# A gated feed-forward layer's up products on one core: the sigmoid goes ahead of the next unit's gate levels, and ScalarE makes the sigmoid's whole levels in every second unit

## What is computed

```python
def _L0_ffn_ref(x, w_gate, w_up, w_down):
    def act_qdq(x):                         # 16 bits, one scale for the whole tensor
        scale = jnp.maximum(jnp.max(jnp.abs(x)) / 32767.0, 1e-12)
        return jnp.clip(jnp.round(x / scale), -32768.0, 32767.0) * scale
    def fixed_qdq_u16(x):
        scale = 1.0 / 65536.0
        return jnp.clip(jnp.round(x / scale), 0.0, 65535.0) * scale
    x = act_qdq(x)
    up = act_qdq(x @ lpbq_dequant(w_up).T)
    gate = act_qdq(x @ lpbq_dequant(w_gate).T)
    sig = fixed_qdq_u16(jax.nn.sigmoid(gate))
    gate = act_qdq(gate * sig)
    o = act_qdq(gate * up)
    return o @ lpbq_dequant(w_down).T
```

## Time and profile before

| | |
|---|---|
| median of three runs | 1704.43 us (1702.17 to 1707.84) |
| profiled execution, its own time | 1706.82 us |
| its span in the profile | 1705.0 us |
| stretch of the gate products | about 379 to 447 us |
| stretch of the up products (16 units) | about 449 to 569 us |
| block `go` | about 571 to 629 us |
| mean granted TensorE clock, whole span | 0.848 |

### The profile page before, as it was taken

How to read it: one execution, slowest core, us unless ns; L and a number is a source line. 1 busy time by engine, 2 the same in 40 slices (tenths; PEclk the granted TensorE clock), 3 DMA queues, 4 the chain that set the end, 5 groups by cost and what they waited for, 6 DMA issues and landing times. The chain is left out here.

```text
span 1705.0 us, 29650 instructions
## 1 busy us (share of the span) xinstructions
PE 1293.8 (76%) x8779; PEld 956.2 (56%) x8780; DVE 1082.7 (64%) x1994; ACT 782.0 (46%) x1138; POOL 527.4 (31%) x426
## 2 busy tenths in 40 slices
PE   5779999349865008679969999533249999999996
PEld 3337777234322007526527777432239999999895
DVE  6947777685587784335647778567635555555553
ACT  0545665055555677100447777343424343444441
POOL 1046777000000000100037777244522333333333
PEclk9979999669999558855779999755569999999998
DMA  5000000100122440140002222384622322222221
GB/s 189 1 4 1 0 0 0 56 1 0 55 111 111 170 144 1 29 111 0 0 28 87 86 86 77 102 280 148 209 95 45 49 39 46 44 48 46 46 44 12
DMA packets 64938, 110.87 MB, mean 65 GB/s; under 512 B 9904, under 2 KB 50960, under 8 KB 64240
## 3 DMA queue, kind: packets, MB, share of 16 engines
q1 hardware_dynamic: 50576, 93.27, 17.3%
q0 software_dynamic: 14304, 16.87, 5.7%
HBM read 74.10 MB, written 37.83 MB: 66 GB/s over the span
## 5 line engine op out<-in xcount | busy, mean ns | idle before, releaser
L1810 POOL DMA_INDIRECT out<-ex_yo,ex_mt x78 | 137.3, 1760 | 314.4 <-DVE ex_yo L1785 181.4
L1735 ACT ACTIVATE ex_hT<-ex_ps_h,e_b1T,e_unscale 128x256 f32<-128x256 f32 x312 | 150.5, 563 | 115.9 <-PE ex_ps_h L1693 115.9
L549 PE MATMUL at_ps_s<-c_M,at_xnT_hi 128*128 (+1 forms) x512 | 163.1, 402 | 20.6 <-issue 13.5
L571 PE MATMUL at_ps_y<-c_VW,at_pT_hi 128*128 (+1 forms) x1024 | 171.1, 273 | 1.3 <-DVE main_x_res L669 1.3
L1693 PE MATMUL ex_ps_h<-ex_xT_hi,e_w_hi 128*128 128x256 f16 x624 | 171.1, 274 | 0.0
L1693 PE MATMUL ex_ps_h<-ex_xT_lo,e_w_hi 128*128 128x256 f16 x624 | 171.0, 274 | 0.0
L1693 PE MATMUL ex_ps_h<-ex_xT_hi,e_w_lo 128*128 128x256 f16 x624 | 171.0, 274 | 0.0
L1706 PE MATMUL ex_ps_y<-e_w_hi,ex_hT_lo 128*128 x624 | 170.1, 273 | 0.0
L1706 PE MATMUL ex_ps_y<-e_w_lo,ex_hT_hi 128*128 x624 | 170.1, 273 | 0.0
L1706 PE MATMUL ex_ps_y<-e_w_hi,ex_hT_hi 128*128 x624 | 170.1, 273 | 0.0
L641 DVE TENSOR_REDUCE at_mx<-at_sc 128x16 f32<-128x960 f32 (+1 forms) x96 | 80.0, 861 | 116.3 <-ACT at_sc L602 116.3
(11 more groups left out here) (273 smaller groups left out, 2914.0 us busy)
## 6 DMA issues: line engine op xcount, KB each, us to landing
at_half<-in_L_ffn_W SPq DMA_DIRECT2D x32, 512.0 KB, 3.6
rt_stage<-in_L_ffn_W SPq DMA_DIRECT2D x32, 512.0 KB
up_scratch<-gm_stg SPq DMA_DIRECT2D x16, 768.0 KB, 3.2
gm_stg<-up_scratch SPq DMA_DIRECT2D x16, 768.0 KB, 4.3
ex_row<-xs SPq DMA_DIRECT2D x39, 258.0 KB, 2.7
main_x_res<-in_x SPq DMA_DIRECT2D x8, 512.0 KB, 12.2
out<-main_x_res SPq DMA_DIRECT2D x4, 1024.0 KB
xs<-rt_pad SPq DMA_DIRECT2D x18, 129.0 KB
```

The costliest lines, as they stand in the source:

```text
L549: last = nc.tensor.matmul(ps_s[j][:, c * CH:(c + 1) * CH], a[:, d, :], b[:, d, bass.ds(off + c * CH, CH)], start=(n == 0), stop=(n == 3 * ...
L571: last = nc.tensor.matmul(ps_y[:, 0:D], a[j][:, n, :], b[:, bass.ds(off + n * D, D)], start=(n == 0 and i == 0), stop=(n == NP - 1 and i = ...
L1735: last = nc.scalar.activation(hT[:, n, :], ps_h[:, n, :], ACT.Relu, bias=b1T[:, bass.ds(e * HT + n, 1)], scale=unscale[:, 0, bass.ds(e, 1)])
L1810: nc.gpsimd.indirect_dma_start(out=acc[:, :], out_offset=bass.IndirectOffsetOnAxis(ap=mt[j][:, q, 1:2].bitcast(U32), axis=0), in_=yo[j][:, ...
```

## The change

ScalarE's order in the up products becomes up_out(u), sigmoid(u), in odd units `sig_levels(u)`, levels(u+1). `sig_levels` exists twice now: on VectorE for even units, as before, and on ScalarE for odd units, as a Copy of `unit(u)` with a constant scale of 65536 to `sq[1]`, without the explicit minimum, reported by a semaphore of its own, `sqa_r`. The product waits for `sq_r` in even units and for `sqa_r` in odd ones, with counts that go up once in two units.

```diff
+            sqa_r = z.sem("sqa_r")
...
+                def sig_levels(u):
+                    act.wait_ge(sig_r, u + 1)
+                    nc.scalar.activation(sq[u % 2][:, :], unit(u), ACT.Copy, scale=65536.0).then_inc(sqa_r, 1)
+
...
                 for u in range(NU):
                     up_out(u)
+                    sigmoid(u)
+                    if u % 2:
+                        sig_levels(u)
                     if u + 1 < NU:
                         levels(u + 1)
-                    sigmoid(u)
...
                 def product(u):
-                    dve.wait_ge(sq_r, u + 1)
+                    dve.wait_ge((sq_r, sqa_r)[u % 2], u // 2 + 1)
...
                 for u in range(NU):
                     up_max(u)
-                    sig_levels(u)
+                    if u % 2 == 0:
+                        sig_levels(u)
                     if u:
                         prod_max(u - 1)
                     product(u)
```

## The result

The changed kernel took 1676.45 us as the median of three runs (1675.28 to 1678.9), against 1704.43 before: a ratio of 0.9836 with a 95% interval of 0.9805 to 0.9868. It is faster, by 28.0 us. The profiled execution took 1675.28 us, its span is 1673.4 us.

The account below looks back on a forecast made before the run. It took a 7.40 us per-unit loop of waits across engines in the up products as the bound; saving 2.8 + 25.1 + 0.9 = 28.8 us from the 1704.43 us median gave 1675.6 us, range 1671 to 1684.

Parts of the forecast that it names:

- The loop of one unit: Up products before the change: waits from gate levels through sigmoid, sigmoid levels, product maximum and product, 7.40 us a unit.
- VectorE is the limit at 10.86 us for two units: Up products after the change: six instructions at 1.665 us plus one sigmoid-level at 0.87, 5.43 us a unit.
- two-unit loops of 7.9 and 8.9 us: Longest waits across engines after the swap: 7.9 us for odd u+1, 8.9 for even, both below VectorE's two-unit work.
- ScalarE is 0.6 us short of it: Up products: ScalarE's gate levels, up_out and sigmoid twice plus one copy need 10.3 us for two units, against VectorE's 10.86.
- The copy takes 1.57 us: ScalarE's new sigmoid-level Copy: 1.57 us, low end 1.52, high end 2.85 with a 1.28 us table load.
- TensorE and the stores are hidden: Up products: matmul groups of 4.06 us and stores of 3.2 us, one every 5.4 us, cost nothing.
- The sum: 2.8 + 25.1 + 0.9 = 28.8 us: Along VectorE in the up products: savings of 2.8 us at the start, 25.1 in the middle, 0.9 at the end.
- All of it reaches the end: Later stages start behind a barrier, so the whole 28.8 us carries to the kernel's end, giving 1675.6 us.
- Rival 1: Up products: costlier copy or hand-offs make ScalarE the limit, 11.6 us for two units, some 1681 us; chance 0.06.
- Rival 2: Up products: TensorE at 1.2 GHz, 7.69 us a group, only 4 us saved, 1700.5 us; chance 0.04.
- Rival 3: Second attention stage: started earlier, it runs at half the clock; 40 us of such work gives 1716 us; chance 0.02.
- Rival 4: Up products: gate levels behind the copy hold up the bank hand-off, only 7 us won, 1697 us; chance 0.03.

Follow-up runs that it names:

- the order alone: Against the kernel before: sigmoid(u) placed ahead of levels(u+1) on ScalarE, VectorE keeping all 16 sigmoid levels; stage 96.78 us, median 1676.03 us, ratio 0.9846.
- the move alone: The changed kernel with ScalarE's old order, levels(u+1) ahead of sigmoid(u), odd units' sigmoid levels still on ScalarE; stage 111.58 us, median 1690.26 us, ratio 0.9932.
- every third unit on VectorE: The changed kernel with VectorE making sigmoid levels only in units 0, 3, ..., 15, ScalarE in the others; stage 90.98 us, ratio 0.9812.
- even units shared with GpSimd: The changed kernel with even units' sigmoid levels split, GpSimd making the first 768 columns, VectorE the last 768; stage 89.42 us, ratio 0.9809.

## Why the prediction was right

1. *The loop of one unit is the limit.* Right. With the order alone changed it is gone (96.78 us), with it kept it stands (111.58 us).
2. *Afterwards VectorE is the limit at 10.86 us for two units.* Right: 10.84 us without idle time, up maxima 5.86 and 4.98 us apart. The two-unit loops of 7.9 and 8.9 us weren't tested by themselves.
3. *ScalarE is 0.6 us short of it.* Right in the sum: 0.50 us of idle time in two units, and a second copy cost 0.87 us of its 1.5. But two terms were off and cancelled, which is luck. The prediction charged nothing for the copy's wait for the sigmoid just ahead of it, "the sigmoid waits that way for the gate levels today". It doesn't: `sigmoid(u)` waits for gate levels u, which ScalarE made a unit earlier, and not for the gate levels u+1 just ahead of it. In the rows above the copy starts 510.31 - 508.71 = 1.60 us after the sigmoid, where it was taken as 1.47, and gate levels start 511.70 - 510.31 = 1.39 us after the copy, where it was taken as 1.5. With only the first off, ScalarE would have had 0.1 us less of its 0.6 us.
4. *The copy takes 1.57 us.* Wrong by 0.09, without effect on the sum, since ScalarE isn't the limit: it took 1.48, below the low end of 1.52 that I gave. The table load of the high end didn't come: the stage has one, ahead of the first sigmoid. The Trainium skill (ScalarE: Activation LUTs, "What ACT_TABLE_LOAD costs") gives 186 ns + 0.833 ns a column for immediate scale and bias and some 93 ns more for each scale or bias read from memory; an estimate from it is 1.47 us for this copy, and the trace agrees (1.48, against 1.56 to 1.58 for gate levels with a scale from memory).
5. *TensorE and the stores are hidden.* Right. No up_out in the stage had idle time ahead of it, so none waited for a store or for matmuls. All 13 groups behind the first three took 4.06 us. One pair of rows from TensorE's timeline, to set beside the earlier trace rows:

```profile
508.86 4.06 PE L934 MATMUL gm_bank<-f_xq,f_WuT 128*128 x18 [0.83 <-ACT gm_stg L972]
514.82 4.06 PE L934 MATMUL gm_bank<-f_xq,f_WuT 128*128 x18 [1.90 <-ACT gm_stg L972]
```

   The Trainium skill's rule on the clock (TensorE: Matmul & The Clock Gate, "A second HAM failure mode: psum-queue depth-cycling") fits the kernel before, where 4 of 13 groups were slow, but isn't borne out after the change: with idle times of 0.22 to 1.90 us between groups that take turns at the banks, none of the 13 groups was slow.
6. *The sum: 2.8 + 25.1 + 0.9 = 28.8 us.* The stage is 28.82 shorter. By parts, counted from gate levels 0: the up maximum of unit 2 starts 2.76 us earlier (17.45 before, 14.69 now), the 13 units take 96.11 - 70.92 = 25.19, and the end 5.98 - 5.11 = 0.87.
7. *All of it reaches the end.* It did: 28.0 us between the first medians. That the median of 1676.45 lies only 0.9 us from the forecast is in part luck, since on the other chips the same kernel had medians of 1669.11 to 1675.05 and gains of 25.4 to 30.9 us; the stage is the sharper test. The 2.5 us more in the span of the trace arose in later stages (the down products took 1.0 us less, the stretch from them to the end of the second attention 1.3 less), where the change does nothing; the spread of the runs is as large.

Rival 1 (ScalarE becomes the limit) didn't occur; a second copy and a copy in every unit each brought it about. Rival 2's price of 1700.5 us was for a case that wasn't run: it counts 13 groups and leaves the first three at 2.4 GHz, as they ran before (54 matmuls in 11.82 us). With all 16 at 7.77 us the kernel is slower (1.0039), so a low clock from the first group on would have cost more than the rival charges. That this clock didn't come is shown by two windows, up to TensorE's last group and behind it (columns of the earlier trace rows): the clock was 1.00 as long as there were matmuls.

```profile
449.00:523.00 74.00, 57.82 (x260) 24.05 (x258) 70.25 (x46) 72.25 (x51) 0.00 (x0) 1.00 0.37 149
523.00:540.00 17.00, 0.77 (x4) 0.16 (x2) 16.97 (x11) 9.94 (x7) 0.00 (x0) 0.60 0.23 93
```

Rival 3 (a later stage at a lower clock) isn't seen in any of the four traces of the change: the second attention has a granted clock of 1.00 in every window of 20 us from 900 to 1040 us, and ends some 1052 us into the first of them. Rival 4 (the change doesn't do what it says) falls with the stage's 28.82 us.

## What to carry to other kernels

When no engine of a stage is saturated, look for the loop that closes across engines, and ask of each member whether the next one needs it or only stands behind it: here an instruction for the *next* unit stood ahead of one that this unit waited for, and swapping the two brought four fifths of the gain for nothing. Then count what each engine needs for the shortest repeating pattern and stop moving work when the sums meet; moving the other eight sigmoid levels to ScalarE as well cost as much here (7 us) as moving the first eight had brought (6 us). Before an idle engine is given work, one such instruction on it should be measured, and a group's mean should be split by shape before it is used as a price.

## What the runs showed of the hardware

- **GpSimd's multiply-and-minimum from f32 to uint16 is slow, and slower beside a product.** It took 2.79 us for 768 columns (3.6 ns a column) while VectorE did reductions. For 1536 columns it took 5.42 us (3.5 ns a column) the one time when VectorE's product wasn't running, and 6.95 us the 15 times when one product of 1.76 us ran beside it; 1.53 us more, nearly the product's length. The product started first, by some 0.05 us (481.55 against 481.60), and kept its 1.76 us. The Trainium skill (SBUF — State Buffer, "Who interferes with whom") says that a VectorE instruction with two inputs from SBUF contends with a GpSimd instruction that reads SBUF, and that the order of issue decides which one is held up. The traces fit that; what happens when GpSimd starts well ahead of a product, no run here shows.
- **The drop to 1.2 GHz came only after longer idle times, and not after each of them.** In the kernel before it followed 3.25 us of idle time, but of the eight groups of that stage with 3.25 or 3.42 us ahead of them only four were slow; two with 3.25 us and two with 3.42 us took 4.06 us. With all sigmoid levels on GpSimd two groups were slow (5.59 and 5.39 us) after 3.05 us, the shortest idle time ahead of a slow group of up matmuls in any trace of this case. With the move alone, TensorE sat idle for 4.15 us ahead of nearly every pair of groups, and the 36 matmuls of the pair took 9.63 us, where two groups at 2.4 GHz take 8.1:

```profile
491.54 9.63 PE L934 MATMUL gm_bank<-f_xq,f_WuT 128*128 x36 [4.15 <-ACT gm_stg L972]
```

  In the variants with no more than 1.9 us of idle time ahead of a group (the change, the order alone, every third unit on VectorE, even units shared with GpSimd), no group was slow.
- **ScalarE's copy with a constant scale is 0.08 to 0.1 us shorter than one whose scale is read from SBUF**, at 1536 columns: 1.48 against 1.56 to 1.58 us. The outputs differ too (uint16 against int16), which no run separates.
- **An instruction that waits for the one directly ahead of it on the same engine starts 0.12 to 0.14 us later than one that doesn't.** On ScalarE the copy starts 1.59 to 1.61 us after the sigmoid it waits for, where gate levels that don't need that sigmoid start 1.47 after it; a second copy that waits for the first starts 1.51 after it, where gate levels start 1.39 after a copy. On VectorE the last product maximum, which waits for the product just ahead, starts 1.79 us after it, where other instructions start 1.66 after a product.
